# Attention with experts on one core: half-full score sets in one pair of banks, and the last two slots by halves

## The chip, the cores and the metric

One core of one Trainium2 chip. The metric is the device time of one execution in microseconds (us), and lower is better. The kernel takes four sequences of 1024 rows with 128 features.

## The reference, cut to what matters

```python
def attention_1(x, Wqkv, bqkv, Wr, br):          # 16 heads of 8 features
    xh = x.reshape(4, 1024, 16, 8).transpose(0, 2, 1, 3)
    q, k, v = split(einsum('bhce,ef->bhcf', xh, Wqkv) + bqkv, 3)
    att = einsum('bhqe,bhke->bhqk', q, k) / sqrt(8)
    att = softmax(att * tril(ones, k=-1))          # masked scores are 0, not -inf
    return einsum('bhqk,bhke->bhqe', att, v).reshape(4, 1024, 128) @ Wr + br

def block_2(x, ...):
    q = k = rope(x) projected; v = x projected     # 16 heads of 8 features
    attn = softmax(where(causal, q @ k.T / sqrt(8), -inf))
    x1 = layer_norm(x + (attn @ v) @ Wo.T + bo) * w1 + b1
    gates = softmax(x1 @ Wg.T + bg); the best two of 8 experts, with their gates
    moe = sum over the two of gate * (x1 @ expert.T + expert_b)
    return layer_norm(x1 + moe) * w2 + b2

x = x + attention_1(_layernorm(x), ...)
x = x + block_2(_layernorm(x), ...)
```

## The kernel before, in words

**Slots, passes, sets, units.** An attention of one sequence is a slot, (a, b) with a the attention (0 or 1) and b the sequence. `SLOTS` (L35) orders the eight: (0,0) (0,1) (1,0) (0,2) (1,1) (0,3) (1,2) (1,3). A slot has eight passes: query half `qh` 0 with its four groups of four heads, then query half 1 with the same (L66). In a pass, each key tile of 128 rows that the 512 queries see is a column block; `sets_of` (L42) packs them: whole sets hold 512 columns of each of four heads, the last set of each pass only 256 (a "half set"). A pass of query half 0 has two whole sets and a half set, one of query half 1 six and a half set. The exponential works on units of 128 x 1024 elements: a whole set is two units (heads 0 and 1, heads 2 and 3), a half set is one. That makes 72 units a slot and 576 in all, of 256 whole sets and 64 half sets.

**Banks.** PSUM holds three pairs of score banks, a bank for accumulated values (`acc`) and one for everything else (`side`). Set g writes the pairs 2g and 2g+1 modulo 3 (`pair`, L94). A half set also writes four banks, 256 columns in each, and its one exponential reads both pairs.

**The loop on TensorE** (`slot`, L1252): for each set g the scores (`scores_set`, L1167, four matmuls of 32 x 128 weights in four row groups, one for each head), side work of the even point, the values of set g-3 (`value_group`, L1191, four heads in four column groups, into `acc`), side work of the odd point. The scores of set g wait for the first exponential of set g-1:

```python
                    pe.wait_ge(probs_raw, FIRST_UNIT[g - 1] + 1)      # L1179
```

**ScalarE** (L1359 to L1384) runs the exponentials (L1378) in order, and between them copies `acc` to `num` (L1300) once for each of the 64 passes, when the pass's values are done three sets later. **GpSimd** masks the diagonal blocks (L1454). **SP** loads queries and keys of a pass (L837, L843) from DRAM up to `LEAD` = 10 units ahead into a ring of three, and runs the stores and loads of the stages.

**Side work** is everything else: p1 (norm and projections for attention 0), p2 (output of attention 0, norm, rotary positions, projections for attention 1, and the bound on the scores: `norm`, `top`, `tops`, `roots`, `shift`), p3 (output of attention 1, norm, gates, the two best experts, e0 and e1 for the eight experts of each row tile, the last norm). A planner (`schedule`, L317) fixes at build time at which point of which set every job stands. It steps through the sets with a clock for each engine (`JOB_TIMES`, `TURN_TIMES`), sorts the jobs by the time by which they are due (`ends`, times `UNIT_TIME` a unit), and places a TensorE job when its inputs are done by these clocks. A p2 job is placed at once; a p1 or p3 job only if TensorE is ahead of the exponential by enough (`ahead` + its time within `LATE`) or if it is due (L422 to L424). All engines then execute the same plan in order. What isn't placed by the end of the loop goes into the tail (`AFTER`), where the score banks serve as side banks too. Each p3 half of 512 rows depends on the halves before it through shared buffers (`p3`, L247).

**Flags.** The shift that keeps the exponentials in range comes from a bound. If a bound doesn't hold, a flag turns the slot to another path (`exact`); each slot begins with that check on TensorE, VectorE and SP (L1275, L993, L1934). The inputs here don't set a flag.

## Time and profile before

| | |
|---|---|
| median of 3 runs | 795.78 us (795.67 to 799.67) |
| the profiled execution | 796.04 us, its span 794.3 us |
| mean granted TensorE clock | 0.954 of full speed |
| TensorE busy | 651.4 us (82%) |
| ScalarE busy | 654.6 us (82%) |
| VectorE, GpSimd busy | 394.4 us (50%), 321.0 us (40%) |
| first exponential starts, last ends | 27.24 us, 720.3 us |
| bytes moved by DMA | 109.79 MB |

Engines in the profile: PE is TensorE's matmuls, PEld its weight loads, ACT ScalarE, DVE VectorE, POOL GpSimd, SP the queue of the loads and stores. L1378 is line 1378 of the kernel before. The times of a group are its busy time and the mean duration of one instruction; "idle before" is the time that its engine stood idle just before instructions of the group, with what ended it. A busy engine is only a limit if nothing else sets the pace, and durations of neighbours overlap, so starts say more than durations.

### The profile page before, as it was taken

How to read it: one execution, taken by the hardware profiler on the slowest of the kernel's cores; microseconds unless marked ns; L12 is line 12 of the kernel's file. 1: busy time of each engine (PE TensorE's matmuls, PEld its weight loads, DVE VectorE, ACT ScalarE, POOL GpSimd, SP SyncE). 2: the span in 40 equal slices, each digit the busy share in tenths (PEclk: the TensorE clock that was granted, in tenths of full speed). 3: DMA queues.
4: the chain of work that ended last, by engine and by line, in shares of the span. 5: the costliest groups of instructions: out<-in, count | busy, mean ns of one | idle time of the engine just before them, and what ended most of it. 6: DMA issues, size and time to landing. Idle time of an engine off the chain costs nothing. (4 is left out here: it accounts for less than half of the span.)

```text
span 794.3 us, 15432 instructions
## 1 busy us (share of the span) xinstructions
PE 651.4 (82%) x5560; PEld 245.9 (31%) x5560; DVE 394.4 (50%) x1089; ACT 654.6 (82%) x748; POOL 321.0 (40%) x635
## 2 busy tenths in 40 slices
PE   4588997888799889889988888888978888977753
PEld 3233332333233233233322322223322332323421
DVE  5364453346446643376455633465544522545575
ACT  1589899998798789999889999998879989895341
POOL 3252336215633325334643344435633344333244
PEclk9699999999999999999999999999999999999776
DMA  7856457644667414434545533423635243300010
GB/s 181 276 190 209 135 163 242 200 122 161 205 211 242 160 53 126 134 108 129 186 132 160 173 114 119 135 77 125 204 120 176 93 135 111 109 27 14 1 40 28
DMA packets 76993, 109.79 MB, mean 138 GB/s; under 512 B 13784, under 2 KB 28256, under 8 KB 76896
## 3 DMA queue, kind: packets, MB, share of 16 engines
q1 hardware_dynamic: 72944, 107.32, 42.8%
q10 hardware_dynamic: 3952, 1.30, 0.7%
q8 instruction: 46, 0.75, 0.4%
q14 instruction: 51, 0.42, 0.2%
HBM read 60.91 MB, written 47.68 MB: 137 GB/s over the span
## 5 line engine op out<-in xcount | busy, mean ns | idle before, releaser
L1378 ACT ACTIVATE probs<-scores,shift 128x1024 f32<-128x1024 f32 x576 | 596.5, 1125 | 70.0 <-PE scores L1183 64.4
L1454 POOL TENSOR_SCALAR_AFFINE_SELECT probs<-probs 128x256 f32<-128x256 f32 (+1 forms) x448 | 195.7, 453 | 366.1 <-ACT probs L1378 365.5
L1212 PE MATMUL acc<-probs,v 128*9 128x512 f32 (+3 forms) x3072 | 318.9, 503 | 4.1 <-ACT num L1300 4.1
L1183 PE MATMUL scores<-qs,ks 32*128 32x512 f32 (+3 forms) x1536 | 159.1, 428 | 74.9 <-ACT probs L1378 72.9
L1183 PEld LDWEIGHTS scores<-qs,ks 32*128 32x128 f32 x1536 | 72.4, 187 | 272.5 <-ACT probs L1378 208.2
L1212 PEld LDWEIGHTS acc<-probs,v 128*9 128x9 f32 x3072 | 58.9, 100 | 105.2 <-issue 66.7
L1501 DVE TENSOR_TENSOR prod<-side,G 128x512 f32<-128x512 f32 x41 | 28.3, 691 | 84.3 <-PE side L1165 84.2
L1165 PE MATMUL side<-we,x1T 128*128 128x512 f32 x92 | 53.0, 659 | 0.7 <-DVE part L1550 0.7
L1435 POOL TENSOR_TENSOR moe<-psum 128x256 f32<-128x256 f32 x32 | 25.0, 781 | 67.6 <-DVE psum L1501 55.3
L1300 ACT ACTIVATE num<-acc 128x512 f32<-128x512 f32 x64 | 38.6, 603 | 5.7 <-PE acc L1212 5.6
L1410 POOL TENSOR_TENSOR rstd<-rstd,expo 128x4 f32<-128x4 f32 x32 | 33.3, 1041 | 2.7
L1335 ACT ACTIVATE probs<-scores,G 128x128 f32<-128x128 f32 x60 | 16.7, 392 | 20.7 <-PE scores L1165 9.4
L1534 DVE COPY xT<-side 128x512 f32<-128x512 f32 x22 | 15.2, 690 | 19.9 <-PE side L1038 17.1
L1549 DVE TENSOR_SCALAR part<-side,binqk 128x512 fp32r<-128x512 f32 x16 | 12.0, 751 | 21.2 <-PE side L1044 17.3
L1165 PE MATMUL scores<-we,x1T 128*128 128x512 f32 x36 | 22.5, 739 | 0.0
L1549 DVE TENSOR_SCALAR part<-side,bqk 128x512 fp32r<-128x512 f32 x12 | 9.0, 751 | 27.1 <-PE side L1044 27.0
L1509 DVE BATCH_NORM_STATS2 stats<-xrow 128x6 f32<-128x128 f32 x72 | 15.6, 278 | 13.2 <-DMA xrow<-in_x 11.2
L1165 PEld LDWEIGHTS side<-we,x1T 128*128 128x128 f32 x92 | 14.5, 194 | 22.7 <-issue 18.8
L1044 PE MATMUL side<-xT,win 128*128 128x512 f32 x32 | 18.0, 645 | 2.1 <-DVE part L1550 2.1
L1409 POOL TENSOR_SCALAR rstd<-mv 128x4 f32<-128x4 f32 x32 | 8.4, 262 | 22.6 <-DVE mv L1512 22.5
L1436 POOL TENSOR_TENSOR moe<-moe 128x128 f32<-128x128 f32 x32 | 15.6, 487 | 2.5
L1501 DVE TENSOR_TENSOR psum<-prod 128x512 f32<-128x512 f32 x20 | 15.3, 765 | 2.6
(193 smaller groups left out, 605.6 us busy)
## 6 DMA issues: line engine op xcount, KB each, us to landing
ks<-k_dram SPq DMA_DIRECT2D x96, 256.0 KB, 4.2
q_dram<-part SPq DMA_DIRECT2D x64, 256.0 KB, 3.2
qs<-q_dram SPq DMA_DIRECT2D x64, 256.0 KB, 3.7
num_dram<-num SPq DMA_DIRECT2D x60, 256.0 KB, 2.7
k_dram<-part SPq DMA_DIRECT2D x30, 256.0 KB, 3.6
xrow<-in_x SPq DMA_DIRECT2D x16, 256.0 KB, 4.5
nat<-num_dram SPq DMA_DIRECT2D x15, 256.0 KB
rdenb<-rden_dram SPq DMA_DIRECT2D x15, 256.0 KB
```

The lines of the kernel that those rows point to most:

```text
L1044: signal(pe.matmul(out[:, :], w[:, int(name == "k"), :], xT[a][:, a or j, :], start=True, stop=True), last)
L1165: signal(pe.matmul(out[:, :], x1T[i // TH][:, i % TH, :], we[:, first:first + HALF], start=True, stop=True), last)
L1183: ins = pe.matmul(scores[:, pair(g, h // 2), h % 2, col:col + w], ks[u][r, kt // TH, (kt % TH) * P:(kt % TH + 1) * P], qs[u][r, q0:q0 + w] ...
L1212: ins = pe.matmul(acc[h * VW:h * VW + VC, q0:q0 + w], v9[V_OF[k]][:, kt, :, HG * hg + h], src, start=(s == 0), stop=last, skip_group_check ...
L1300: act.activation(num[gp % 2][:, :], acc[:, :], ACT.Copy).then_inc(acc_read, 1)
L1335: ins = act.activation(products(b, i, c)[:, e, :], src[:, e * D:(e + 1) * D], ACT.Copy, scale=G[i // TH][:, i % TH, NE // 2 * c + e:NE // ...
L1378: act.activation(dst, src, ACT.Exp, bias=shift[:, column(k):column(k) + 1], scale=SCALE).then_inc(probs_raw, 1)
L1410: pool.tensor_tensor(r, r, expo[:, 0:1].broadcast_to(list(r.shape)), ALU.pow).then_inc(root_ready[w], 1)
L1435: link(pool.tensor_tensor(moe[:, :, :], psum4[:, i % 2, 0:2, :], psum4[:, i % 2, 2:4, :], ALU.add))
L1454: ins = pool.affine_select(out=blocks, in_=blocks, compare_op=ALU.is_ge, fill=0.0, base=a - 1, pattern=[[0, blocks.shape[1]], [1, P]], cha ...
L1501: return dve.tensor_tensor(out, in0, in1, op)
L1549: link(dve.tensor_scalar(pt[:, c, 0, :], src, bias[:, c:c + 1], None, ALU.add))
```

## The change

1. The pair is chosen by unit and no longer by set: unit n uses pair n % 3. A half set takes one pair: heads 0 and 1 in columns 0 to 255 of its two banks, heads 2 and 3 in columns 256 to 511. Heads 0 and 2 share a bank, so TensorE writes them one after the other: heads 0 and 1 at the set's usual place, then the values of set g-3, then (behind a wait for the first two, `half_scores`) heads 2 and 3. No side job stands between. A set waits for the exponential of its last unit less three.
2. The last two slots are cut into halves that take turns. `STRETCHES` lists whole slots 0 to 5, then (6, half 0), (7, half 0), (6, half 1), (7, half 1). Ten flag checks in place of eight. The last sequence gets two bounds, one for its first 512 rows and one for all (`BOUNDS`: five in place of four), so one more `top`, `tops`, `roots`, `shift`. p3 takes its last four halves of rows in this order too (`rows_half`).
3. The planner: its clocks follow the new order of TensorE's work, due times are by stretch, `UNIT_TIME` is 1.1 in place of 1.15, `LATE` 0.2 in place of 0.5, and `ahead` is measured to where ScalarE would be out of work.

The diff, cut to its core:

```diff
+STRETCHES = [(k, (0, 1)) for k in range(NSLOT - 2)] + [(k, (qh,)) for qh in range(2) for k in (NSLOT - 2, NSLOT - 1)]
...
-def pair(g, i):
-    return (2 * g + i) % PAIRS
...
+def rows_half(b, j):
+
+    order = [(SLOTS[k][1], qh) for k, halves in STRETCHES if SLOTS[k][0] for qh in halves]
+    return order[2 * b + j]
...
+BOUNDS = [(b, 0) for b in range(B)] + [(B - 1, 1)]
...
+def last_by(k, b, j):
+
+    return at(k + 2, 40 * j) if b < B - 2 else NU - 12 * (2 * B - 2 - 2 * b - j) if not (b == B - 1 and j) else at(k + 2, 40)
...
-        ends[x("parts_out")] = ends[x("v")] = at(k, -12)
+        ends[x("parts_out")] = ends[x("v")] = STRETCH_FIRST[stretch_of(k, j)] - 12
...
-        ends[x("store")] = at(k + 2, 40 * j)
+        ends[x("store")] = last_by(k, b, j) + 40
...
-UNIT_TIME = 1.15
-LATE = 0.5
+UNIT_TIME = 1.1
+LATE = 0.2
...
+    def next_scores(g):
+
+        if g + 1 == SETS_ALL:
+            return 0.0
+        return 0.44 if len(UNITS_OF[g + 1]) > 1 else 0.3 + values(g + 1)
...
-            if g:
-                clock["PE"] = max(clock["PE"], exps[FIRST_UNIT[g - 1]] + 0.1)
...
+            if units[-1] >= PAIRS:
+                clock["PE"] = max(clock["PE"], exps[units[-1] - PAIRS] + 0.1)
+            clock["PE"] += 0.22 * len(units) if len(units) > 1 else 0.15
...
-            ahead = t + (0.49 * len(UNITS_OF[g - LAG]) if p % 2 == 0 and g >= LAG else 0.0) - exps[FIRST_UNIT[g]] - 0.1
+            ahead = t + (values(g) if p % 2 == 0 else 0.0) + next_scores(g) + 0.08 - clock["ACT"]
...
+        def place_of(g, h):
+
+            units = UNITS_OF[g]
+            if len(units) == 1:
+                return units[0], h % 2, HALF // 2 * (h // 2)
+            return units[h // 2], h % 2, 0
...
             def scores_set(g, shifted):
...
+                elif last >= PAIRS:
+
+                    pe.wait_ge(probs_raw, last - PAIRS + 1)
+                if is_half(qh, s):
+                    heads_scores(g, (0, 1), shifted).then_inc(half_scores, 1)
                 else:
-
-                    pe.wait_ge(probs_raw, FIRST_UNIT[g - 1] + 1)
...
+                    heads_scores(g, range(HG), shifted).then_inc(scores_ready, 1)
+
+            def other_heads(g, shifted):
+
+                pe.wait_ge(half_scores, HALVES_TO[g])
+                heads_scores(g, (2, 3), shifted).then_inc(scores_ready, 1)
...
+            def stretch(st, shifted):
+                for g in range(STRETCH_GROUP[st], STRETCH_GROUP[st + 1]):
                     scores_set(g, shifted)
                     for x in DURING[2 * g]:
                         turn(*x)
                     if g >= LAG:
                         value_group(g - LAG)
+                    if len(UNITS_OF[g]) == 1:
+                        other_heads(g, shifted)
                     for x in DURING[2 * g + 1]:
                         turn(*x)
...
-                if len(UNITS_OF[g]) == 1:
-                    low_, high = sorted((pair(g, 0), pair(g, 1)))
-                    src = scores[:, low_:high + 1:high - low_, :, 0:HALF // 2]
-                    dst = probs[n % NPB][:, :, :].rearrange("p a (c s) -> p a c s", c=2)
-                else:
-                    src = scores[:, pair(g, n - FIRST_UNIT[g]), :, :].rearrange("p c s -> p (c s)")
-                    dst = probs[n % NPB][:, :, :].rearrange("p c s -> p (c s)")
-                act.activation(dst, src, ACT.Exp, bias=shift[:, column(k):column(k) + 1], scale=SCALE).then_inc(probs_raw, 1)
+                src = scores[:, n % PAIRS, :, :].rearrange("p c s -> p (c s)")
+                dst = probs[n % NPB][:, :, :].rearrange("p c s -> p (c s)")
+                act.activation(dst, src, ACT.Exp, bias=shift[:, column(st):column(st) + 1], scale=SCALE).then_inc(probs_raw, 1)
```

## Rows read from the trace of the kernel before

**Rows 1.** The page's busy time of each engine, with share of the span and instructions.

```profile
PE 651.4 (82%) x5560; PEld 245.9 (31%) x5560; DVE 394.4 (50%) x1089; ACT 654.6 (82%) x748; POOL 321.0 (40%) x635
```

**Rows 2.** Table by stage: length, then busy time (and instructions) of PE, PEld, DVE, ACT, POOL.

```profile
27.20:720.30 693.10, 594.82 (x5350) 213.93 (x5354) 330.86 (x892) 625.92 (x657) 286.71 (x573) 0.97 0.47 149
720.30:794.30 74.00, 42.80 (x158) 23.15 (x150) 47.79 (x148) 24.85 (x84) 27.15 (x47) 0.76 0.08 22
```

**Rows 3.** Groups of instructions, ScalarE: busy us, mean ns, idle before and its releasers.

```profile
L1378 ACT ACTIVATE probs<-scores,shift 128x1024 f32<-128x1024 f32 x576 | 596.5, 1125 | 70.0 <-PE scores L1183 64.4 <-issue 4.2
```

**Rows 4.** Timeline of ScalarE: start us, length us, merged instructions, [idle before, releaser].

```profile
33.46 2.12 ACT L1378 ACTIVATE probs<-scores,shift 128x1024 f32<-128x1024 f32 x2 [0.99 <-PE scores L1183]
...
168.82 2.12 ACT L1378 ACTIVATE probs<-scores,shift 128x1024 f32<-128x1024 f32 x2 [0.70 <-PE scores L1183]
...
337.32 0.60 ACT L1300 ACTIVATE num<-acc 128x512 f32<-128x512 f32 x1 [0.23 <-PE acc L1212]
337.82 8.14 ACT L1378 ACTIVATE probs<-scores,shift 128x1024 f32<-128x1024 f32 x8
...
706.61 5.13 ACT L1378 ACTIVATE probs<-scores,shift 128x1024 f32<-128x1024 f32 x5 [0.70 <-PE scores L1183]
```

**Rows 5.** Timeline of TensorE, in the same columns.

```profile
168.27 0.51 PE L1183 MATMUL scores<-qs,ks 32*128 32x512 f32 x4
...
303.40 1.12 PE L1165 MATMUL side<-we,x1T 128*128 128x512 f32 x2
304.45 0.51 PE L1183 MATMUL scores<-qs,ks 32*128 32x512 f32 x4
304.89 1.06 PE L1212 MATMUL acc<-probs,v 128*9 128x512 f32 x8
305.87 0.93 PE L1160 MATMUL side<-be,GT 8*128 8x128 f32 x6
...
308.49 0.39 PE L1183 MATMUL scores<-qs,ks 32*128 32x256 f32 x4 [0.24 <-ACT probs L1378]
308.81 0.63 PE L1212 MATMUL acc<-probs,v 128*9 128x256 f32 x8
309.37 1.13 PE L1165 MATMUL side<-we,x1T 128*128 128x512 f32 x2
```

**Rows 6.** Groups by shape in the loop: the score matmuls of half sets.

```profile
L1183 PE MATMUL scores<-qs,ks 32*128 32x256 f32 x256 | 25.5, 386 | 16.1 <-ACT probs L1378 16.1
```

**Rows 7.** Table by stage, instructions on `side` alone: PE, PEld, DVE, ACT.

```profile
27.20:720.30 693.10, 163.13 (x770) 85.31 (x770) 142.22 (x223) 0.00 (x0) 0.97 0.47 149
```

**Rows 8.** Timeline: jobs of the last sequence, and the first exponential of slot 6.

```profile
520.03 1.16 PE L1102 MATMUL side<-wr,attT 128*128 128x128 f32 x8
...
546.48 2.12 ACT L1378 ACTIVATE probs<-scores,shift 128x1024 f32<-128x1024 f32 x2 [1.01 <-issue]
...
568.28 0.46 PE L1059 MATMUL side<-headsum,sq 128*128 128x16 bf16 x12
...
613.75 0.55 PE L1066 MATMUL side<-ident,nrm 128*128 128x128 f32 x3
...
624.28 0.27 PE L1077 MATMUL side<-sh,ones 1*128 1x1 f32 x2
...
722.73 1.05 PE L1102 MATMUL scores<-wo,attT 128*128 128x128 f32 x8
```

**Rows 9.** Groups of instructions in the tail (720.3 to 794.3): expert matmuls.

```profile
L1165 PE MATMUL scores<-we,x1T 128*128 128x512 f32 x36 | 22.5, 739 | 0.0
...
L1165 PE MATMUL side<-we,x1T 128*128 128x512 f32 x10 | 6.9, 780 | 0.0
```

**Rows 10.** The page's costliest groups: all score matmuls.

```profile
L1183 PE MATMUL scores<-qs,ks 32*128 32x512 f32 (+3 forms) x1536 | 159.1, 428 | 74.9 <-ACT probs L1378 72.9
```

**Rows 11.** Timeline where ScalarE waits longest in the first half of the loop.

```profile
275.57 0.47 PE L1059 MATMUL side<-headsum,sq 128*128 128x16 bf16 x12 [2.44 <-POOL sq L1418]
...
278.65 2.12 ACT L1378 ACTIVATE probs<-scores,shift 128x1024 f32<-128x1024 f32 x2 [3.35 <-PE scores L1183]
```

More of the change, by code:

```diff
@@ L149, in takes, with stretch_of, pass_of, bound_of @@
     return sum(turn_time(x)[1:])
+def stretch_of(k, qh):
+    return next(st for st, (k_, halves) in enumerate(STRETCHES) if k_ == k and qh in halves)
+def pass_of(k, i):
+    return next(gp for gp in range(NP) if PASS_OF[gp][1] == k and (PASS_OF[gp][2], PASS_OF[gp][3]) == PASSES[i])
+def rows_half(b, j):
+    order = [(SLOTS[k][1], qh) for k, halves in STRETCHES if SLOTS[k][0] for qh in halves]
+    return order[2 * b + j]
+BOUNDS = [(b, 0) for b in range(B)] + [(B - 1, 1)]
+def bound_of(k, halves):
+    qh = halves[0]
+    b = SLOTS[k][1]
+    return BOUNDS.index((b, qh if b == B - 1 else 0))
+def bound_tiles(n):
+    return TH if n == B - 1 else T
 def at(slot, unit):
-    return slot * UB + unit
+    return (STRETCH_FIRST[stretch_of(slot, 0)] if slot < NSLOT else NU + (slot - NSLOT) * UB) + unit
 def slot_of(a, b):
@@ L256, in p3 @@
         k = slot_of(1, b)
-        out[x("load")] = [("p2", b, "keep", j), x("out", 1)]
+        rows = rows_half(b, j)
+        out[x("load")] = [("p2", rows[0], "keep", rows[1]), x("out", 1)]
         out[x("pre")] = [x("load")]
@@ L274, in p3 @@
         out[x("bias")] = [x("GT"), last("moe", 2)]
-        out[x("load2")] = [("p2", b, "keep", j)] + ([] if alone else [x("scale2", 1)])
+        out[x("load2")] = [("p2", rows[0], "keep", rows[1])] + ([] if alone else [x("scale2", 1)])
         out[x("x2")] = [x("load2")]
@@ L395, in finish, with exponentials, values @@
         done[x] = begin + dve + 0.1
+    def exponentials(units):
+        for n in units:
+            clock["ACT"] = max(clock["ACT"], clock["PE"] + 0.08) + 1.0
+            exps[n] = clock["ACT"] + 0.12
+            for gp in range(NP):
+                if evacuated(gp) == n:
+                    clock["ACT"] += 0.48
+                    done[("evacuated", gp)] = clock["ACT"] + 1.5
+    def values(g):
+        return 0.49 * len(UNITS_OF[g - LAG]) if g >= LAG else 0.0
+    def next_scores(g):
+        if g + 1 == SETS_ALL:
+            return 0.0
+        return 0.44 if len(UNITS_OF[g + 1]) > 1 else 0.3 + values(g + 1)
     for p in range(NPOINT):
@@ L1063, in project @@
                     out = start_job(job)
-                    job_read((work, b, "norm", 1))
+                    job_read((work, b, "norm", j if b == B - 1 else 1))
                     for i in range(3):
@@ L1069, in project @@
                     out = start_job(job)
-                    job_read((work, b, "top", 0))
+                    job_read((work, b, "top", j))
                     for i in range(3):
```

358 lines of the change are left out of this document (195 added, 163 removed).

## The prediction

> **What bounds the kernel now.** I began with the page: TensorE and ScalarE are both busy for 82% of the span [rows 1], and neither share says which one sets the time, so I cut the span where the work changes. The table by stage [rows 2] has three parts: 27.2 us ahead of the first exponential, a loop of 693.1 us with all 576 exponentials (27.20 to 720.30), and a tail of 74.0 us. In the loop ScalarE is busy 625.9 us and TensorE 594.8 us; in the tail no engine passes 47.8 us of 74.0.
>
> The group of the exponentials [rows 3] says what ScalarE does. One is listed with 1125 ns, but neighbours overlap: eight in a row take 8.14 us and two 2.12 us [rows 4], so each adds 1.00 us, and about 0.11 us of a run is its last one's end. A copy of acc, of which there are 64, adds 0.49 us (337.32 to 337.82). The floor by ScalarE is 576 x 1.0047 + 64 x 0.49 = 610 us, and the other 83 us of the loop's 693.1 are something else. The group's own columns say what: 70.0 us idle before exponentials, 64.4 us of it released by score matmuls.
>
> Where are these waits? ScalarE's timeline [rows 4] shows a pattern that repeats with every half set. The half set's exponential ends, and only then may TensorE write the next set, as the half set lies in both of its pairs and the next set needs one of them (L1179 waits for it). At 168.27 the scores start [rows 5], at 168.82, after 0.70 us idle, the exponential [rows 4]. There are 63 such places (the 64th half set is the last), the first at 33.46, the last at 706.61. I measured each from start to start, less 1.0047 us per exponential and 0.49 us per copy: the 31 behind a half set of query half 1 have a median of 1.04 us and sum to 31.5 us, the 32 behind one of query half 0, where the copy of acc fills part of the gap, sum to 19.0 us. Together that is 50.5 us. The other 32.8 us are spread over the rest, single large ones among them.
>
> **Part 1, banks by unit.** With pair n % 3 for unit n, a half set takes one pair. The set behind it waits for the exponential before the half set's, so its scores (0.55 us from their start to the exponential's, 168.27 to 168.82) fit beneath the half set's own 1.00 us. The 50.5 us go. From below the gain is bounded by nothing, from above by 50.5.
>
> What comes late instead is the half set itself. Its scores are now in two parts with the value matmuls of three sets before between them, and ScalarE gets it only after the second part. From the release by exponential n-3 to the start of n there are 2 x 1.00 us. Needed are the first part, the values, the second part and the lead to the exponential: from TensorE's timeline [rows 5] a half set's four score matmuls take 0.32 us from start to start (308.49 to 308.81), the values of a whole set 0.98 (304.89 to 305.87). The price of a part of two matmuls isn't in the trace. A whole set takes 0.44 (304.45 to 304.89) and a half set 0.32, so 256 columns make 0.12 and 0.20 stays whatever the width. A part costs between 0.12 and 0.32; I take 0.32, the nearest row, for the first. The lead from the second part's start to the exponential is 0.43 (0.55 less the 0.12 of the missing 256 columns). That is 0.32 + 0.98 + 0.43 = 1.73 us, and 0.27 us are to spare; with 0.12 for the first part 0.47.
>
> The Trainium skill, TensorEngine Tiling (Array Packing), Key Properties, says that changing the tiling mode, not just the tile, drains TensorE. By that rule the 0.20 is paid when scores (32 rows) turn to values (32 columns), and a second part followed by another set's scores would pay only 0.12. The rows agree with a fixed part at such a turn; none shows scores behind scores. By the rule the extra TensorE time below is 7.7 us and not 20.5, which makes the sum up to 12.8 us smaller where TensorE sets the pace and leaves it where ScalarE does.
>
> Is TensorE there in time? Before a half set it waits 16.1 us in all [rows 6], 0.25 us per half set, and that wait is for exponential n-2. The new release is one exponential (1.00) earlier, so with the same side jobs in front TensorE comes 0.75 us after it, and the exponential is 0.48 us late (0.28 with the larger spare). Over 64 half sets: 30.7 or 17.9 us given back, and nothing if the planner keeps side jobs away from these places; its edit (LATE 0.5 to 0.2, `ahead` measured against ScalarE's clock) does so for the p1 and p3 jobs alone. I take 0.35 us, a little under the middle of 0.48 and 0.28: 22.4 us back.
>
> The same sum for TensorE's whole load: 256 whole sets x (0.44 + 0.98) = 363.5, 64 half sets x (0.32 + 0.56, 308.81 to 309.37) = 56.3, and 163.1 us of side jobs in the loop [rows 7]; 583 us. The second parts add 64 x 0.12 to 64 x 0.32 = 7.7 to 20.5, hence 591 to 604 us against ScalarE's 610. So TensorE is nearly as full as ScalarE at its floor, which is why I keep the loop's other 32.8 us as they are and take no more than 28 us net. Loop: 693.1 - 50.5 + 22.4 = 665.0 us.
>
> Edits at nothing: the masks and value matmuls of half sets only read other columns (the 1024 elements are the same); the tenth and ninth flag checks sit where TensorE waits for an exponential (the slot boundary at 546.48 idles 1.01 us [rows 8], no more than another place behind a half set); if that cover is gone, 2 x 0.3 us, an estimate from what such a boundary has beyond 0.70. The fifth bound adds top, tops and shift once: TensorE 0.55 + 0.27 us for top and shift, as much again for tops, and a few small VectorE steps on an engine busy 330.9 of 693.1 us.
>
> **Part 2, the order of the last two slots.** Half 0 of batch 3 is attended 20 units into slot 6 and no longer 72, so its keys and its shift are due at 546.48 + 20 units (about 23 us), 569 to 570. Before, its norm ran at 568.28 and the bound's chain from top to shift took 613.75 to 624.28, 10.5 us [rows 8]. Left where it was it would be 10 us late. But its input (the `out` job at 520.03) had come 48 us ahead of that norm, with p3 jobs between; due times are written into the plan, so I count nothing, and 10 us as the upper bound. Its stores to DRAM are issued by SP before the loads of that stretch, as now.
>
> In return the second p3 half is ready 32 units earlier, the third at the same place. The tail before starts with half (3,0) still at its `out` (722.73 [rows 8]) and does 36 + 10 of the expert matmul instructions, two to a job: 23 jobs of 64 [rows 9]. Side jobs in the last two slots are limited by TensorE's room, which shrinks with the gaps, so fewer ready jobs is what the order cures and less room what part 1 costs. Bounds: 7 jobs less at two instructions of 0.74 us each, about 10 us off (tail 64; with the chain a little shorter 60), or six more jobs, tail 80. I take 4 us off: 70.0.
>
> **Sum.** 27.2 + 665.0 + 70.0 = 762.2 us of span. The profiled run lasted 1.74 us longer than its span (796.04 and 794.30) and lies 0.26 above the median of 795.78: 763.9, and 764 against the median.
>
> **Rivals.** *TensorE has room after all* (12%). Nothing is returned at the half sets: loop 642.6, tail 62, time 733. For it: its 74.9 us idle before score matmuls [rows 10]. Against it: the demand above. The Trainium skill, Perfetto Trace Analysis, Identifying the Most-Contended Engine, speaks for this one: matmul busy time is not a good measure of how full TensorE is, and weight-load busy time is. That time is 31% of the span here [rows 1]. The trace bears it out only so far, since start-to-start times, which no model of ends enters, still fill 583 of 693 us.
>
> *TensorE takes over* (13%). Side inputs come late on an engine that executes in order: in the loop before, one norm job waited 2.44 us for POOL's squares and ScalarE then stood 3.35 us [rows 11]. With 0.48 us at each half set and two more such stalls, 30.7 + 6.7 us come back, and jobs pushed out make the tail 80: 27.2 + 680.0 + 80 = 787.2, time 789. A third of this case lies within 0.5%.
>
> *Slower* (5%): the half set's second part is the new choke. If TensorE comes to each half set one more side job late (1.05 us, 303.40 to 304.45 [rows 5]), its exponential is 0.48 + 1.05 = 1.53 us late, 97.9 us in all for the 50.5 saved: 27.2 + 740.5 + 74, time 843. It decides from a mean lateness of 0.85 us per half set. Against it: the planner counts those jobs.
>
> *The set behind a half set isn't released earlier* (2%), because the wait is really another one, such as the loads of keys: no change, 796.
>
> **How the numbers follow.** The forecast has 68%. A difference under 0.5% (792 to 800) is about what a measurement of this kernel can tell from none. Faster: 68 + 12 + 9 = 89%; same: 4 + 2 = 6%; slower 5%. The range takes in a return between 0 and 39 us and a tail between 62 and 78: 736 to 789 leaves out most of the first rival, some of the second and all of the slower one, 2 in 10.
>
> **What would show it.** Right: the idle time before exponentials falls from 70.0 to some 40 us; the starts behind a half set have no gap; half of what is left stands right before half sets; TensorE's wait before the 256-wide scores is near nothing; loop 655 to 675. Wrong: gaps of 0.7 us still behind half sets (rival four), a loop under 650 (rival one), over 680 (rival two), or stalls of several us where stretch (7, half 0) begins; a tail beyond 62 to 78.

## The result, and the profile after

The changed kernel takes 813.03 us (median of 4 runs, 810.83 to 820.32) beside 797.72 of the kernel before (4 runs, 795.67 to 802.9): a ratio of 1.0197, 95% interval 1.0156 to 1.0237. I had forecast 764 us, faster. The profiled run lasted 813.96 us, its span is 812.2.

The busy time of each engine, from the page of the kernel after, answers to [rows 1]:

```profile
PE 680.7 (84%) x5568; PEld 260.7 (32%) x5568; DVE 395.7 (49%) x1115; ACT 650.4 (80%) x733; POOL 323.6 (40%) x635
```

The table by stage, loop and tail (columns as in [rows 2]), and then the instructions on `side` alone, as in [rows 7]:

```profile
30.07:745.70 715.63, 630.04 (x5390) 232.06 (x5394) 339.92 (x935) 627.09 (x659) 293.91 (x581) 0.95 0.44 143
745.70:812.20 66.50, 35.59 (x130) 19.41 (x122) 39.08 (x128) 19.57 (x67) 22.60 (x39) 0.73 0.07 20
...
30.07:745.70 715.63, 177.22 (x802) 91.94 (x802) 147.49 (x231) 0.00 (x0) 0.95 0.44 143
```

The costliest groups of the page, answering to [rows 3, 10]:

```profile
L1482 ACT ACTIVATE probs<-scores,shift 128x1024 f32<-128x1024 f32 x576 | 600.7, 1125 | 85.9 <-PE scores L1291 83.1
...
L1316 PE MATMUL acc<-probs,v 128*9 128x512 f32 (+3 forms) x3072 | 324.6, 511 | 14.4 <-ACT num L1407 14.3
L1291 PE MATMUL scores<-qs,ks 32*128 32x512 f32 (+3 forms) x1536 | 182.7, 435 | 40.4 <-ACT probs L1482 39.5
```

The head is 2.9 us longer, the loop 22.5 longer, the tail 7.5 shorter: 17.9 of span (794.3 to 812.2). The head says nothing on the change: over the profiled runs of this document it lies between 26.6 and 30.1 us, and `fall_after` below, with the change in it, has 27.3. ScalarE has the same work in the loop (625.9 and 627.1 us busy); what grew is its idle time before exponentials, 70.0 to 85.9, although TensorE's wait for exponentials fell from 72.9 to 39.5. The banks do release TensorE earlier, and ScalarE still gets its scores later. The 16.1 us that TensorE waited before the scores of half sets [rows 6] are gone, as forecast; the same group in the loop after:

```profile
L1291 PE MATMUL scores<-qs,ks 32*128 32x256 f32 x256 | 50.9, 392 | 0.3 <-ACT probs L1482 0.2
```

Measured by starts, as in the prediction (start to start, less 1.0047 us per exponential and 0.49 per copy), the loop's excess moved like this:

| us | behind a half set | right before one | elsewhere | sum |
|---|---|---|---|---|
| before | 50.5 | 5.6 | 27.1 | 83.3 |
| forecast | 0 | 28.0 | 27.1 | 55.1 |
| after | 14.7 | 41.0 | 50.2 | 105.9 |

Taken instruction by instruction from the same traces, a column of this table or of the next moves by up to 2.3 us, and the sums stay; read the columns no finer than that.

**Before a half set.** The timeline of ScalarE in the kernel after (start, length, [idle before, releaser]), around a half set of query half 0. The half set is the last of the three exponentials at 313.40; it starts at 315.56, 0.15 us late. The 0.64 us ahead of the row are a whole set's and count as elsewhere:

```profile
310.59 2.17 ACT L1482 ACTIVATE probs<-scores,shift 128x1024 f32<-128x1024 f32 x2
313.40 3.28 ACT L1482 ACTIVATE probs<-scores,shift 128x1024 f32<-128x1024 f32 x3 [0.64 <-PE scores L1291]
316.58 0.59 ACT L1407 ACTIVATE num<-acc 128x512 f32<-128x512 f32 x1
```

and that of TensorE around the same half set:

```profile
312.84 0.51 PE L1291 MATMUL scores<-qs,ks 32*128 32x384 f32 x8
313.28 1.06 PE L1316 MATMUL acc<-probs,v 128*9 128x384 f32 x16
314.27 0.38 PE L1291 MATMUL scores<-qs,ks 32*128 32x256 f32 x2
314.58 0.63 PE L1316 MATMUL acc<-probs,v 128*9 128x256 f32 x8
315.14 0.38 PE L1291 MATMUL scores<-qs,ks 32*128 32x256 f32 x2
315.45 1.12 PE L1257 MATMUL side<-we,x1T 128*128 128x512 f32 x2
```

A part of two score matmuls takes 0.31 us from start to start (314.27 to 314.58, 315.14 to 315.45), about as long as four took before (0.32): the end of the range that I took. Where no side job follows and the next set's scores stand right behind, it is less; TensorE in the kernel after, a second part and four scores of the next set as one row of six:

```profile
128.44 0.63 PE L1316 MATMUL acc<-probs,v 128*9 128x256 f32 x8
129.00 0.61 PE L1291 MATMUL scores<-qs,ks 32*128 32x256 f32 x6
129.54 1.16 PE L1142 MATMUL side<-wqkv,xT 128*128 128x128 f32 x8
```

0.54 us for six, that is 0.10 more than the 0.44 of the four alone.

How late are the half sets? By single instructions the median of the 64 is 0.36 us, and 58 of them sum to 25.4. The other six are over 1.5 us each and make 15.4 together; the two largest, 3.77 and 4.29, stand behind a late input of the second kind below.

**Elsewhere** single large waits grew: eight of over 1.5 us make 23.7 us, where the loop before had two with 7.0. The worst is in the last stretches. Timelines of VectorE, TensorE and ScalarE in the kernel after, in this order, cut to the chain:

```profile
616.22 0.69 DVE L1605 TENSOR_TENSOR psum<-prod 128x512 f32<-128x512 f32 x1
622.42 0.42 DVE L1605 TENSOR_TENSOR rope<-xn,cos 128x256 f32<-128x256 f32 x1 [5.51 <-issue]
...
623.88 0.69 DVE L1638 COPY xT<-side 128x512 f32<-128x512 f32 x1
```

```profile
618.78 0.51 PE L1291 MATMUL scores<-qs,ks 32*128 32x512 f32 x4 [0.23 <-ACT probs L1482]
624.63 2.07 PE L1257 MATMUL side<-we,x1T 128*128 128x512 f32 x2 [5.34 <-DVE xT L1638]
```

```profile
617.62 3.12 ACT L1482 ACTIVATE probs<-scores,shift 128x1024 f32<-128x1024 f32 x3 [0.18 <-PE scores L1291]
627.75 0.60 ACT L1407 ACTIVATE num<-acc 128x512 f32<-128x512 f32 x1 [7.01 <-PE acc L1316]
```

VectorE stands for 5.51 us and waits for nothing the profile shows ("issue"), just behind the start of stretch (6, half 1), whose first exponential runs at 615.29: it loads the flag and branches over the exact path. Its copy to xT is late, TensorE (in order) stands 5.34 us before an expert matmul, the values and scores behind that are late, and ScalarE stands 7.01 us. The matmul pair then takes 2.07 us, where the one at 315.45 takes 1.12. The table by stage around it, kernel after, says why (the column ahead of the last two is the granted clock):

```profile
614.00:624.00 10.00, 4.74 (x42) 1.50 (x40) 4.32 (x11) 6.56 (x7) 3.64 (x8) 0.92 0.49 148
624.00:630.00 6.00, 5.34 (x24) 1.33 (x25) 2.54 (x5) 2.25 (x3) 0.00 (x0) 0.57 0.12 43
630.00:636.00 6.00, 6.00 (x48) 2.53 (x51) 3.09 (x11) 5.49 (x6) 1.98 (x6) 1.00 0.37 103
```

Behind TensorE's pause the clock is at its lower level (0.57 in the mean, 1.2 GHz for most of the 6 us). Such stands of VectorE come at every start of a slot or stretch but the first, where VectorE waits for a load anyway: seven in the loop before (2.72 to 4.13 us, 23.4 in all), nine in the loop after (2.67 to 5.51, 32.6). The longest of the seven, from VectorE's timeline of the kernel before:

```profile
204.79 0.69 DVE L1501 TENSOR_TENSOR xrow<-xrow,br 128x512 f32<-128x512 f32 x1 [4.13 <-issue]
```

Not every stand marked "issue" is a check: one of 6.79 us at 589.6 in the kernel before is still there, with 6.80, in `noflag_before`, which has no checks on VectorE.

A second kind of late input is the one of [rows 11], and it hides in another column: the exponential at 573.74 is a half set's, so its wait counts as right before one, and so does one of 3.77 us at 406.1 behind the same job. TensorE's timeline after, and ScalarE's:

```profile
571.23 0.47 PE L1151 MATMUL side<-headsum,sq 128*128 128x16 bf16 x12 [2.87 <-POOL sq L1522]
```

```profile
573.74 1.11 ACT L1482 ACTIVATE probs<-scores,shift 128x1024 f32<-128x1024 f32 x1 [4.19 <-PE scores L1291]
```

### The profile page after: what moved, and what is told of

Read it like the earlier page. It is cut to its first block and busy times, and to the rows that moved or that the text cites. A ratio compares the mean times of both kernels' runs of the same rounds, so it can differ in the third digit from the quotient of the medians.

```text
span 812.2 us, 15473 instructions
## 1 busy us (share of the span) xinstructions
PE 680.7 (84%) x5568; PEld 260.7 (32%) x5568; DVE 395.7 (49%) x1115; ACT 650.4 (80%) x733; POOL 323.6 (40%) x635
## 5 line engine op out<-in xcount | busy, mean ns | idle before, releaser
L1482 ACT ACTIVATE probs<-scores,shift 128x1024 f32<-128x1024 f32 x576 | 600.7, 1125 | 85.9 <-PE scores L1291 83.1
L1558 POOL TENSOR_SCALAR_AFFINE_SELECT probs<-probs 128x256 f32<-128x256 f32 (+1 forms) x448 | 199.3, 461 | 408.4 <-ACT probs L1482 408.3
L1316 PE MATMUL acc<-probs,v 128*9 128x512 f32 (+3 forms) x3072 | 324.6, 511 | 14.4 <-ACT num L1407 14.3
L1291 PE MATMUL scores<-qs,ks 32*128 32x512 f32 (+3 forms) x1536 | 182.7, 435 | 40.4 <-ACT probs L1482 39.5
L1291 PEld LDWEIGHTS scores<-qs,ks 32*128 32x128 f32 x1536 | 83.5, 191 | 253.1 <-ACT probs L1482 163.3
L1605 DVE TENSOR_TENSOR prod<-side,G 128x512 f32<-128x512 f32 x45 | 31.1, 691 | 78.5 <-PE side L1257 73.1
L1257 PE MATMUL side<-we,x1T 128*128 128x512 f32 x96 | 58.3, 692 | 9.1 <-DVE xT L1638 5.5
L1442 ACT ACTIVATE probs<-scores,G 128x128 f32<-128x128 f32 x52 | 14.4, 387 | 21.7 <-PE scores L1257 11.5
L1613 DVE BATCH_NORM_STATS2 stats<-xrow 128x6 f32<-128x128 f32 x72 | 15.6, 278 | 13.9 <-DMA xrow<-in_x 10.1
L1653 DVE TENSOR_SCALAR part<-side,bqk 128x512 fp32r<-128x512 f32 x12 | 9.0, 750 | 25.0 <-PE side L1136 22.4
L1653 DVE TENSOR_SCALAR part<-side,binqk 128x512 fp32r<-128x512 f32 x16 | 12.0, 750 | 18.0 <-PE side L1136 17.9
L1257 PE MATMUL scores<-we,x1T 128*128 128x512 f32 x32 | 19.4, 732 | 0.0
L1605 DVE TENSOR_TENSOR psum<-prod 128x512 f32<-128x512 f32 x22 | 15.6, 708 | 2.9
L1136 PE MATMUL side<-xT,wqkv 128*128 128x512 f32 x24 | 14.5, 686 | 2.6 <-DVE part L1654 2.6
L1630 DVE SCALAR_TENSOR_TENSOR x<-y,rstd,l1b 128x128 f32<-128x128 f32 x28 | 11.5, 470 | 10.2 <-POOL rstd L1514 10.2
```

Source lines behind the costliest of these rows:

```text
L1136: signal(pe.matmul(out[:, :], w[:, int(name == "k"), :], xT[a][:, a or j, :], start=True, stop=True), last)
L1257: signal(pe.matmul(out[:, :], x1T[i // TH][:, i % TH, :], we[:, first:first + HALF], start=True, stop=True), last)
L1291: ins = pe.matmul(dst, ks[u][r, kt // TH, (kt % TH) * P:(kt % TH + 1) * P], qs[u][r, q0:q0 + w], start=True, stop=not shifted)
L1316: ins = pe.matmul(acc[h * VW:h * VW + VC, q0:q0 + w], v9[V_OF[k]][:, kt, :, HG * hg + h], src, start=(s == 0), stop=last, skip_group_check ...
L1482: act.activation(dst, src, ACT.Exp, bias=shift[:, column(st):column(st) + 1], scale=SCALE).then_inc(probs_raw, 1)
L1558: ins = pool.affine_select(out=blocks, in_=blocks, compare_op=ALU.is_ge, fill=0.0, base=a - 1, pattern=[[0, blocks.shape[1]], [1, P]], cha ...
```

## The experiments

Ratios are to the kernel before, run on the same chip alongside; loops, tails and excesses (measured as in the table above) are from the one profiled run of each (that of `p1_oldplan`, 808.1, is its slowest; that of `halfcost`, 808.4, lies 6 us above its median). The two narrow kernels ran once each.

| | us (median) | ratio, 95% | loop | tail | behind / before half / else |
|---|---|---|---|---|---|
| p1_oldplan | 803.2 | 1.0020 [0.9985, 1.0055] | 705.5 | 73.6 | 19.5 / 43.6 / 32.8 |
| p1_newplan | 795.5 | 0.9938 [0.9906, 0.9969] | 697.7 | 70.2 | 9.8 / 39.8 / 38.5 |
| p2_alone | 800.5 | 0.9982 [0.9940, 1.0024] | 706.2 | 65.7 | 56.4 / 6.2 / 33.9 |
| halfcost | 802.5 | 1.0022 [0.9983, 1.0061] | 721.7 | 57.8 | 16.9 / 55.7 / 39.5 |
| straight | 817.8 | 1.0221 [1.0162, 1.0280] | 724.8 | 65.5 | 31.7 / 15.0 / 68.4 |
| copy_first | 811.4 | 1.0139 [1.0076, 1.0202] | 713.2 | 66.5 | 15.6 / 36.7 / 51.2 |
| narrow_before | 793.1 | one run, none | 693.5 | 70.7 | 51.3 / 5.2 / 27.3 |
| narrow_after | 815.3 | one run, none | 721.4 | 63.6 | 11.5 / 44.6 / 55.6 |
| noflag_before | 792.7 | 0.9930 [0.9905, 0.9954] | 689.6 | 74.2 | 48.9 / 4.2 / 26.9 |
| noflag_p1 | 784.4 | 0.9822 [0.9769, 0.9875] | 685.8 | 70.6 | 6.8 / 41.2 / 28.1 |
| noflag_p2 | 788.8 | 0.9868 [0.9805, 0.9930] | 692.1 | 66.7 | 49.7 / 4.7 / 27.9 |
| noflag_after | 796.2 | 0.9976 [0.9946, 1.0006] | 701.3 | 66.1 | 8.7 / 43.9 / 39.0 |
| noflag_copy_after | 794.6 | 0.9949 [0.9912, 0.9986] | 698.2 | 67.7 | 7.7 / 40.0 / 40.9 |
| copy_first_p1 | 785.8 | 0.9847 [0.9781, 0.9914] | 687.6 | 70.9 | 9.8 / 40.5 / 27.6 |
| fall_before | 797.2 | 0.9951 [0.9924, 0.9978] | 687.7 | 77.2 | 48.8 / 3.0 / 26.1 |
| fall_after | 800.7 | 1.0013 [0.9985, 1.0041] | 702.8 | 66.5 | 8.6 / 44.7 / 39.8 |
| fall_p1 | 777.4 | 0.9717 [0.9662, 0.9773] | 678.2 | 70.7 | 5.7 / 38.6 / 24.2 |
| sq_fall_after | 781.2 | 0.9771 [0.9735, 0.9808] | 683.2 | 66.2 | 8.8 / 30.2 / 34.5 |

### The parts apart

`p1_oldplan` is the kernel before with the banks alone, its side jobs placed as before:

```diff
-                    pe.wait_ge(probs_raw, FIRST_UNIT[g - 1] + 1)
+                    pe.wait_ge(probs_raw, last - PAIRS + 1)
...
+                    if len(UNITS_OF[g]) == 1:
+                        other_heads(g, shifted)
...
-                    src = scores[:, pair(g, n - FIRST_UNIT[g]), :, :].rearrange("p c s -> p (c s)")
+                src = scores[:, n % PAIRS, :, :].rearrange("p c s -> p (c s)")
```

> Part 1 alone, with the plan of side jobs exactly as in the kernel before (slots whole, due times and clocks of before): only the pair of a unit and the two parts of a half set's scores change. Theory A (TensorE is full: the second parts' 20 us on an in-order engine come back as waits right before half sets and elsewhere): within 10 us of before, 790 to 810, with the 50 us behind half sets gone and 30 to 50 us of new idle ahead of half sets and in between. Theory B (the new plan is what is bad: it places side jobs whose inputs are not there): with the old plan the banks pay, 765 to 780. Theory C (the halves taking turns cost the time): also 765 to 780 here.

`p1_newplan` adds the planner's new clocks:

```diff
-UNIT_TIME = 1.15
-LATE = 0.5
+UNIT_TIME = 1.1
+LATE = 0.2
...
+            ahead = t + (values(g) if p % 2 == 0 else 0.0) + next_scores(g) + 0.08 - clock["ACT"]
```

> Part 1 alone with the planner's new clocks, UNIT_TIME 1.1 and LATE 0.2, slots whole. Theory A: like the run with the old plan, within 8 us of it. Theory B: 15 us or more slower than with the old plan, 800 to 815, with late side inputs as in the changed kernel (some 30 us of TensorE waits for other engines than ScalarE in the loop, 19 before). Theory C: 765 to 780.

`p2_alone` is the order of the last two slots on the old banks and clocks:

```diff
+STRETCHES = [(k, (0, 1)) for k in range(NSLOT - 2)] + [(k, (qh,)) for qh in range(2) for k in (NSLOT - 2, NSLOT - 1)]
```

> Part 2 alone: stretches, the fifth bound and p3 in the order of the halves, with the old pairs of banks and the old planner clocks and constants. Theory A and B: within 8 us of before, the tail 4 to 10 us shorter (as measured in the changed kernel, 66.6 against 74.0) and the last two slots as long as before. Theory C: slots 4 to 7 longer by 15 to 22 us as in the changed kernel, 805 to 815.

The banks alone are worth nothing (1.0020): 31 us less behind half sets, 38 us more before them. With the new clocks they gain 0.6%. The second part alone costs nothing that can be measured, although its loop is 13 us longer, since its tail is 8 us shorter and the profiled run of before (796.0) lies 3 us below the median of the runs alongside (799.1). Apart they come to 0.992 of before, together to 1.020. Some 22 us lie in what the parts do to each other, give or take 5 by the intervals.

`halfcost` gives the planner the half part's measured price:

```diff
-            clock["PE"] += 0.22 * len(units) if len(units) > 1 else 0.15
+            clock["PE"] += 0.22 * len(units) if len(units) > 1 else 0.31
```

> The changed kernel with one correction in the planner: each part of a half set's scores costs 0.31 us (as its trace shows from start to start) in place of 0.15, so 0.62 in place of 0.3 when it looks ahead. The planner's own end of the loop goes from 643 to 663 us. Theory A: no gain from a better estimate, as the load is the same, 805 to 820. Theory B: side jobs move away from half sets and the waits before them shrink by 10 to 20 us, 790 to 803.

It takes 10 us off the changed kernel by the medians (14 by the ratios), though not where it aims: before half sets it gets worse (55.7), and it is the tail that falls from 66.5 to 57.8. The plan as a whole moved, so it says little on the half part's price.

### The half set itself

`straight` puts the second part right behind the first, `copy_first` puts the copy of acc ahead of a half set's exponential:

```diff
                     heads_scores(g, (0, 1), shifted).then_inc(half_scores, 1)
+                    other_heads(g, shifted)
...
-                    if len(UNITS_OF[g]) == 1:
-                        other_heads(g, shifted)
```

> The changed kernel with heads 2 and 3 of a half set right behind heads 0 and 1 (TensorE waits for its own first part), and the values of three sets before behind both, as before the change; same plan. The half set's exponential is ready 0.98 or 0.56 us earlier. Theory D: the waits before half sets fall from 41 to 10 to 20 us, the time to 780 to 800. Theory A: TensorE stands some 0.2 us more at each of 64 places, and what is gained before half sets comes back in between: 805 to 820.

```diff
+                if len(UNITS_OF[g]) == 1:
+                    while e < NP and evacuated(e) <= n:
+                        evacuate(e)
+                        e += 1
                 act.wait_ge(scores_ready, g + 1)
```

> The changed kernel with one edit on ScalarE: where the copy of acc falls on a half set (the 32 of query half 0), it is run ahead of that half set's exponential and not behind it. The three-sets-old values that it copies are now done before the second part of the scores, so ScalarE has it to do while it waits. Theory D (a ring of waits: second part behind the values, exponential behind the second part, copy behind the exponential, the next values behind the copy): TensorE's waits for the copy in the loop fall from 14.3 to under 6 us, the 41 us before half sets by 10 to 16, time 785 to 803. Theory A (TensorE is simply full): no more than 5 us off the changed kernel's 813.

Both times came out where theory A had them. With both parts together the gap before half sets goes (41.0 to 15.0) and comes back behind them (14.7 to 31.7) and elsewhere (50.2 to 68.4). So the place of the second part, behind the values of three sets before, is what makes the half set late, but the other place is no better (1.0221 beside 1.0197, within the intervals): the two parts, the second behind its wait for the first, take 0.76 us from start to start in `straight` (the median), 0.44 more than four matmuls in one go. The copy's wait on TensorE goes as meant, in the page of `copy_first`:

```profile
L1316 PE MATMUL acc<-probs,v 128*9 128x512 f32 (+3 forms) x3072 | 325.7, 512 | 3.4 <-ACT num L1407 3.2
```

That is 11 us less waiting, for 2 us in the median (0.6% by the ratios), and the intervals overlap.

### Is TensorE full?

`narrow_before` and `narrow_after` cut the expert matmuls to 8 columns:

```diff
-    signal(pe.matmul(out[:, :], x1T[i // TH][:, i % TH, :], we[:, first:first + HALF], start=True, stop=True), last)
+    signal(pe.matmul(out[:, 0:8], x1T[i // TH][:, i % TH, :], we[:, first:first + 8], start=True, stop=True), last)
```

> The kernel before with the expert matmuls 8 columns wide in place of 512; it leaves out almost all of the experts' products, everything else keeps its instructions. TensorE is relieved of 0.8 us for each of some 41 jobs in the loop, 33 us. If TensorE's load isn't what makes the waits here, the loop stays at 685 to 693 with the 50 us behind half sets unchanged; the tail gets some 10 us shorter.

> The changed kernel with the same narrow expert matmuls (leaves out almost all of the experts' products). Theory A: with 33 us less on TensorE the waits before half sets and in between fall from 91 us to 50 or less, and the changed kernel is now the faster of the two by 15 to 30 us. Theory D: the waits before half sets stay above 30 us and the PE's waits for the copy above 12, as these sit in the order of the instructions and not in the load; it is no faster than the narrow kernel before by more than 5 us.

Some 28 and 31 us less on `side` (163.1 to 135.6, 177.2 to 146.3) gained nothing in either kernel's loop (693.5 beside 693.1, 721.4 beside 715.6), and the waits before half sets stayed. But the granted clock, the third number from the end, fell in both, from 0.97 and 0.95; the loop of `narrow_before`:

```profile
27.13:720.60 693.47, 578.74 (x5350) 218.39 (x5354) 330.79 (x891) 624.87 (x657) 286.78 (x573) 0.95 0.46 148
```

and that of `narrow_after`:

```profile
28.46:749.90 721.44, 619.40 (x5390) 237.77 (x5394) 341.67 (x938) 627.11 (x659) 296.96 (x581) 0.92 0.45 143
```

So less work and a slower clock came together, and these two runs alone don't decide. The last experiment tells more: there the time falls and TensorE's work stays.

### VectorE's flag checks

Four kernels leave VectorE's checks out:

```diff
-                    with dve.If(dve.value_load(flags[0:1, st:st + 1], min_val=0, max_val=1)):
-                        exact(st)
```

> The kernel before without the flag checks on VectorE (same part left out). Theory F: seven inner boundaries, of which only two are followed by a large wait: 3 to 7 us less, 789 to 796. The gap to the changed kernel without them shrinks from 15 us to 5 to 9. If the checks don't matter: as before, 795 to 801.

> The changed kernel without the flag checks on VectorE (it leaves out that engine's part of the other path, which these inputs never take; TensorE and SP still check). Theory F: at each of the nine inner boundaries VectorE stands 2.7 to 5.5 us with a load, a branch and the jump over the other path's code; its results for TensorE come late a few units later (the largest waits of ScalarE lie 5 to 7 units behind a boundary), the TensorE clock falls, and two boundaries more make more of it. Then the large waits near boundaries go, slow-clock time falls from 73 us to under 60, and the time to 795 to 803. If the checks don't matter: 809 to 816.

> Part 1 with the new planner clocks (795.5 before), without the flag checks on VectorE (same part left out). Theory F: seven boundaries, five of them followed by waits of 1.5 to 4.2 us: 780 to 788, that is faster than the kernel before without its checks by 5 us or more; part 1 pays once side results are in time. If the waits there have another cause: 792 to 798.

> The second part alone (turns of the last two slots' halves on the old banks and old planner clocks) without VectorE's flag checks (left out: the same as in the other runs without them). With checks it took 800.5. Theory: the second part's own cost is its two more checks and their late results, so that without any it shows the gain of its tail: below the kernel before without checks (792.65) by up to 8, 785 to 789. Rival: the cost is the denser side work in the loop, and it stays at or above 792.

These kernels can't take the exact path. The missing checks take off 0.7% before, 1.2% of each part alone (0.9938 to 0.9822, 0.9982 to 0.9868), and 2.2% after. Each part alone is now faster than the kernel before without checks, though the second part's interval overlaps that one's. Two with the copy first:

> Part 1 with the new planner clocks, slots whole, and the copy of acc ahead of a half set's exponential. In the changed kernel that edit gave about 2 us and took TensorE's waits for the copy from 14.3 to 3.2. Here the same: 790 to 795, if small gains add up; it would be the fastest version with all of the computation in it.

> The changed kernel without VectorE's flag checks (left out: VectorE's look at the flag and its recomputation for sequences with a set flag) and with the copy of acc ahead of a half set's exponential. Theory (late inputs meet a TensorE that has no slack): the copy's worth shows once the late inputs are fewer, as in the version with banks alone (-10 there): 796.2 - 8 = 788. Rival (the copy's place is worth what it was with the checks, 811.35 against 813.0): 795.

On the banks alone the copy's place is worth 0.9% by the medians (0.9938 to 0.9847, the intervals overlap), on the whole change 2 us: there the rival held.

Is it the load or the branch of the check? In `fall_p1` (`p1_newplan` with the copy first), `fall_before` and `fall_after` the load stays, and the exact path stands behind the whole loop, as on TensorE, so that nothing is branched over:

```diff
+            with ExitStack() as good_slots:
+                for k in range(NSLOT):
+                    begun[k] = step[0]
+                    dve.wait_ge(flag_ready, FLAG_OF[k] + 1)
+                    dve.reg_mov(flagged, dve.value_load(flags[0:1, k:k + 1], min_val=0, max_val=1))
+                    good_slots.enter_context(dve.If_eq(flagged, 0))
+                    slot(k)
+                    rest(k)
+                tail()
+            with dve.If_ne(flagged, 0):
...
```

> Banks by unit, the new planner clocks, the copy of acc ahead of a half set's exponential (the run at 785.8), and VectorE's flag checks kept but laid out so that the good path falls through: the exact path stands behind the whole loop and VectorE does not branch over it. The load of the flag stays. Complete computation. If the stall at each check is the branch over code: as without checks, 785.8 - 11 = 775 us, and no stand of over 2 us at a slot's start on VectorE. If it is the load of the flag: 786 +- 3, the stands stay. Half and half: 780.

> The kernel before with VectorE's flag checks kept and laid out so that the good path falls through (as in the run at 777.4); nothing else is changed, the computation is complete. Theory (the branch over the exact path is the whole stall): the time without checks, 792.65, so 0.993 of before; no stand of over 2 us on VectorE at a slot's start. Rival (the load costs a part): 795.

> The changed kernel with the same layout of VectorE's checks, nothing else. Theory: the time without checks, 796 (0.998 of before), 17 us below the changed kernel, so that the ten branches were all of the step that I had priced at nothing. Rival (the load costs a part, ten times): 800 to 805.

The same places as above in `fall_after`, VectorE, TensorE and ScalarE:

```profile
606.45 0.69 DVE L1605 TENSOR_TENSOR psum<-prod 128x512 f32<-128x512 f32 x1
608.35 0.43 DVE L1605 TENSOR_TENSOR rope<-xn,cos 128x256 f32<-128x256 f32 x1 [1.20 <-issue]
```

```profile
610.83 1.12 PE L1257 MATMUL side<-we,x1T 128*128 128x512 f32 x2 [1.31 <-DVE xT L1638]
```

```profile
612.58 0.60 ACT L1407 ACTIVATE num<-acc 128x512 f32<-128x512 f32 x1 [1.61 <-PE acc L1316]
```

5.51 is now 1.20, 5.34 is 1.31, 7.01 is 1.61, and the pair of matmuls takes 1.12 us, not 2.07. No slot's or stretch's start in the loop shows a stand of over 2 us any more. The branches over the exact path alone cost the changed kernel 1.8% (1.0197 to 1.0013; in the profiled runs the loop is 12.8 us shorter and the head 2.8) and the one before 0.5%. Leaving the load out too gives 0.4% and 0.2% more by the medians, within the intervals. So the medians, 800.7 and 797.2, came out on the side of the rival (the load has a part in it), but that part isn't clear of the noise. `fall_p1`, with nothing left out, is at 0.9717. Its loop, and its exponentials, waiting 44.5 us for scores where the kernel before waits 64.4:

```profile
27.85:706.08 678.23, 610.09 (x5362) 225.53 (x5362) 332.40 (x908) 624.28 (x657) 293.46 (x574) 0.97 0.47 152
...
L1413 ACT ACTIVATE probs<-scores,shift 128x1024 f32<-128x1024 f32 x576 | 597.6, 1131 | 46.4 <-PE scores L1221 44.5
```

### GpSimd's squares

Without checks the parts apart are 0.9822 and 0.9868, together 0.9976. Measured from `noflag_before` (0.9930) both gains should give 0.976; 17 us are lost between them. TensorE's waits for squares add up to 8.0 us (noflag_p1), 7.3 (noflag_p2) and 12.4 (noflag_after). `sq_fall_after` is `fall_after` with the squares on VectorE:

```diff
-                pool.tensor_tensor(sq[:, 2, :], pt[:, 0, 0, :], pt[:, 1, 0, :], ALU.mult)
-                pool.tensor_tensor(sq[:, 0:2, :], pt[:, :, 0, :], pt[:, :, 0, :], ALU.mult).then_inc(sq_ready, 1)
+                dve.tensor_tensor(sq[:, 2, :], pt[:, 0, 0, :], pt[:, 1, 0, :], ALU.mult)
+                dve.tensor_tensor(sq[:, 0:2, :], pt[:, :, 0, :], pt[:, :, 0, :], ALU.mult).then_inc(sq_ready, 1)
```

> The kernel of fall_after with the eight squares jobs on VectorE in place of GpSimd, complete computation. Without checks on VectorE the two parts apart are 0.9822 and 0.9868 of before and together 0.9976, so 17 us are lost between them; TensorE waits 12.5 us for GpSimd's squares with both, 8.0 and 7.3 with either. Theory (the late squares carry much of it): TensorE waits under 2 us for squares and the time falls from 800.7 by 8 to 12, to about 790. Rival (what the two parts cost each other is TensorE's load): the waits go, other waits of TensorE for ScalarE grow by as much, and the time stays within 3 us of 800. The other way it could fail: VectorE gets 2 us more per job and other inputs come late instead.

The view of the one line, the norm's matmuls: in `fall_after`

```profile
L1151 PE MATMUL side<-headsum,sq x96: 169/169/183, 123.7 to 634.6; 128*128 128x16 bf16 x96
its engine sat idle before it (us, times) until:
  POOL sq L1522: 12.4, 5
```

and in `sq_fall_after`, where no wait is listed:

```profile
L1151 PE MATMUL side<-headsum,sq x96: 169/169/193, 121.6 to 617.2; 128*128 128x16 bf16 x96
its engine sat idle before it (us, times) until:
who waited for it (us, times):
```

The loop of `fall_after`, then the loop and the exponentials of `sq_fall_after`:

```profile
27.31:730.10 702.79, 626.35 (x5390) 231.15 (x5394) 342.53 (x937) 627.13 (x659) 293.91 (x581) 0.96 0.46 146
...
28.36:711.55 683.19, 614.57 (x5390) 228.06 (x5394) 356.79 (x954) 626.34 (x659) 275.12 (x565) 0.98 0.48 150
...
L1482 ACT ACTIVATE probs<-scores,shift 128x1024 f32<-128x1024 f32 x576 | 600.2, 1128 | 57.7 <-PE scores L1291 55.4
```

The waits for squares are gone, and the time falls by 19.5 us, more than the 8 to 12 expected. That is about as much as the parts had cost each other, but it isn't shown to be the same time: squares came late in each part alone too, and neither the parts nor the kernel before were run with the squares on VectorE. 14.5 of it were right before half sets (44.7 to 30.2), 5.3 elsewhere. Part of it is the clock (0.96 to 0.98 in the loop; TensorE's busy time falls from 626.3 to 614.6 for the same 5390 matmuls): in `fall_after` the granted clock averaged 0.50 to 0.73 over some 6 us behind four of the five waits for squares (123.7, 395.0, 447.0, 562.6), and 1.00 behind the shortest (184.1, 1.05 us). A job's two products take 3.2 us on GpSimd and 2.1 on VectorE, and there (busy 342.5 us of the loop, now 356.8) they made nothing late that shows.

## Why the prediction was wrong

Of the 50 us by which the span missed (812.2 for 762.2), 14.7 are behind half sets, 13.0 right before them, 23.1 elsewhere in the loop and 2.9 in the head; the tail gave 3.5 back.

**Gap behind half sets, 50.5 us to nothing:** right in kind. 14.7 us are left, 8.6 once the branches are gone.

**Price of a two-matmul part, 0.12 to 0.32, taken 0.32:** right, 0.31. The Trainium skill's rule on tiling modes (TensorEngine Tiling (Array Packing), Key Properties), which I weighed there, says that changing the tiling mode, and not just the tile, drains TensorE. The trace agrees with it: 0.10 to 0.12 us for a second part with scores right behind it (25 rows of six in the loop, ten of them at 0.54 to 0.56, most others at 0.8 with a wait in between), 0.31 where another kind of matmul follows.

**Returned right before half sets, 0.35 us each, 22.4 in all:** right as a price, too small as a sum. The median half set is 0.36 us late, but 35.4 us came on top of the 5.6 that were there, as six single waits make 15.4. Without late branches and squares, in `sq_fall_after`, 30.2 us are left where 28.0 were forecast, with a median of 0.34. `straight` shows that the place behind the values is the mechanism. So most of the surplus belongs to the next step.

**"I keep the loop's other 32.8 us as they are":** the step that failed. Right before half sets apart, 27.1 us became 50.2. My reason was capacity, 591 to 604 us of TensorE against 610 of ScalarE. In fact most of what came on top were late inputs into an engine that executes in order: the two repairs, branches and squares, take the ratio from 1.0197 to 0.9771. My explanation for the growth is that the gaps behind half sets had been TensorE's slack too; closing them, and moving the last sequence's jobs, left fewer places to absorb a late input. The branches fit it, 3.9 us before and 14.7 after, though there are two more of them; for the squares it is argued. I had the list of these gaps and did not ask who was late in them.

**"The tenth and ninth flag checks sit where TensorE waits for an exponential ... 2 x 0.3 us":** failed. I looked at the check on TensorE, which falls through, and not on VectorE, which branches over the exact path. VectorE stands 2.7 to 5.5 us at nine of the ten, and at the place shown the lateness reached ScalarE five units later. The trace of before had seven such stands in its loop, each marked "issue". Measured: 14.7 us of the changed kernel (1.0197 to 1.0013, give or take 4), where the kernel before pays 3.9 (0.9951).

**Part 2, "count nothing, 10 us as the upper bound", tail 70.0:** the tail was better than forecast, 66.5 (its upper bound of 80 was reckoned short: six more jobs at two instructions of 0.74 us are 8.9 and make 83). The late keys that I feared didn't come: stretch (7, half 0) starts at 589.82, 0.24 us late, and the sign named for that, stalls of several us at its start, isn't there; the 7 us stall stands one stretch later and is a branch's. Without checks the second part's loop is 2.5 us longer than the one before (692.1 and 689.6) and its tail 7.5 shorter.

**The rivals:** "TensorE takes over" (13%, 789 us) named the right rows, the norm's wait for squares [rows 11], but with two more such stalls where their effect was 19.5 us, and without the branches. Slower had 5%, by another mechanism (each half set late by one more side job, 1.53 us), which did not come: the mean is 0.64. With both repairs the forecast's own terms stand near: excess 8.8 / 30.2 / 34.5 against 0 / 28.0 / 27.1, and 781 us against 764.

**What stays open.** Sums of repairs are not exact, as each changes what the next absorbs. Whether the squares cost the kernel before as much was not run. That the lower clock multiplied the stalls is read from the traces; no run held the clock fixed. The remaining 34.5 us elsewhere, and why both parts together keep more of them than `fall_p1` (24.2), were not taken apart, and the copy's place together with the squares on VectorE was not tried.

## What to carry to other kernels

When a gap on the bounding engine is closed, list what every in-order engine feeding it waits for elsewhere, and by which engine: those gaps may be the cover for late inputs. Count a check or a branch once for every engine that executes it, and look for stands marked "issue" at the places where the old code has it. Such a repair can be worth more after the tight change than before: the same kind of branch cost 4 us in one kernel (seven in the loop) and 15 in the other (nine).

## What was not expected of the hardware

A check that loads a flag and branches over a long block left VectorE standing 2.7 to 5.5 us; with the block moved out of the way, the same place shows 1.2 us in place of 5.51. No run varied the length of the block. And TensorE's time depends on its pauses: behind a wait of 5.34 us the granted clock averaged 0.57 over 6 us and a pair of matmuls took 2.07 us in place of 1.12, while cutting 31 us of its side work by narrower matmuls (one run) brought the loop's clock from 0.95 to 0.92 and no time.
